# Attention on 64-row halves of the PE array, column tiles that interleave the causal work, and causal masks moved to VectorE and GpSimd

## The reference, cut to what matters

```python
scores = einsum('bqhd,bkhd->bhqk', q, k) / sqrt(8)     # F and H: every query sees every key
attn = softmax(scores); ctx = einsum('bhqk,bkhd->bqhd', attn, v)

attn = einsum('bhql,bkl->bhqk', q_lat, c_kv) / sqrt(8)  # L, causal
attn = where(tril, attn, -inf); attn = softmax(attn)
```

## Time and profile before

| | us |
|---|---|
| three runs | 3379.24, 3382.4, 3384.87; median 3382.4 |
| span of the profiled execution | 3382.5 |
| PE busy | 3032.9 (90%) |
| DVE busy | 2225.2 (66%) |
| ACT busy | 1668.8 (49%) |
| POOL busy | 168.7 (5%) |
| mean granted PE clock | 0.915 |

### The profile page before, as it was taken

How to read it: one execution, slowest core, us unless ns; L and a number is a source line. 1 busy time by engine, 2 the same in 40 slices (tenths; PEclk the granted TensorE clock), 3 DMA queues, 4 the chain that set the end, 5 groups by cost and what they waited for, 6 DMA issues and landing times. The chain is left out here.

```text
span 3382.5 us, 48839 instructions
## 1 busy us (share of the span) xinstructions
PE 3032.9 (90%) x14997; PEld 1205.9 (36%) x14997; DVE 2225.2 (66%) x4191; ACT 1668.8 (49%) x2007; POOL 168.7 (5%) x88
## 2 busy tenths in 40 slices
PE   6788859999999997997799999958999999998998
PEld 2787732222222223443233333322222222222443
DVE  5444459988889893223667666647989888894322
ACT  4212123666666665433255555531666666666333
POOL 1222220000000000001100000011000000000000
PEclk9888866999999997998699999975999999999899
DMA  1000010110011011120111111111010000110211
GB/s 37 1 0 0 0 61 11 29 29 19 27 29 29 17 30 32 69 69 12 59 32 39 30 30 41 30 32 59 15 30 29 29 19 28 29 29 21 76 56 31
DMA packets 75059, 105.46 MB, mean 31 GB/s; under 512 B 17334, under 2 KB 48016, under 8 KB 72433
## 3 DMA queue, kind: packets, MB, share of 16 engines
q1 hardware_dynamic: 71755, 100.97, 9.8%
q10 hardware_dynamic: 3104, 1.94, 0.2%
HBM read 68.72 MB, written 20.55 MB: 26 GB/s over the span
## 5 line engine op out<-in xcount | busy, mean ns | idle before, releaser
L466 DVE TENSOR_REDUCE Hmaxes<-Hm 128x1 f32<-128x512 f32 x1044 | 658.2, 685 | 95.6 <-PE Hm L392 95.0
L466 DVE TENSOR_REDUCE Fmaxes<-Fm 128x1 f32<-128x512 f32 x1044 | 658.1, 685 | 95.5 <-PE Fm L392 95.1
L447 ACT ACTIVATE Hprob<-Hs 128x1024 f32<-128x1024 f32 x512 | 498.5, 1021 | 242.3 <-PE Hs L357 240.7
L447 ACT ACTIVATE Fprob<-Fs 128x1024 f32<-128x1024 f32 x512 | 498.5, 1021 | 242.1 <-PE Fs L357 240.6
L466 DVE TENSOR_REDUCE Lmaxes<-Lm 128x1 f32<-128x512 f32 (+3 forms) x664 | 373.1, 605 | 179.0 <-PE Lm L392 105.3
L447 ACT ACTIVATE Lprob<-Ls 128x1024 f32<-128x1024 f32 (+7 forms) x384 | 293.1, 776 | 268.5 <-PE Ls L360 144.8
L392 PE MATMUL Hm<-Hka,Hqa 99*128 99x512 bf16 x1044 | 381.6, 404 | 27.4 <-DMA Hvh<-Hvstack 11.5
L392 PE MATMUL Fm<-Fka,Fqa 99*128 99x512 bf16 x1044 | 381.4, 404 | 26.8 <-DMA Fvh<-Fvstack 11.0
L357 PE MATMUL Fs<-Fqa,Fka 99*128 99x512 bf16 x1024 | 308.3, 385 | 1.6 <-ACT Fprob L447 1.2
L357 PE MATMUL Hs<-Hqa,Hka 99*128 99x512 bf16 x1024 | 308.2, 384 | 1.6 <-ACT Hprob L447 1.2
L374 PE MATMUL Ho<-Hprob,Hvh 128*32 128x512 f32 x2048 | 276.3, 612 | 0.6 <-ACT Hprob L447 0.6
(11 more groups left out here) (428 smaller groups left out, 2883.7 us busy)
## 6 DMA issues: line engine op xcount, KB each, us to landing
FEwb<-FE_weights SPq DMA_DIRECT2D x8, 1024.0 KB, 5.9
HEwb<-HE_weights SPq DMA_DIRECT2D x8, 1024.0 KB, 5.3
Fqa<-F_qparts SPq DMA_DIRECT2D x51, 96.0 KB
Fka<-F_kparts SPq DMA_DIRECT2D x51, 96.0 KB
Lqa<-L_qparts SPq DMA_DIRECT2D x51, 96.0 KB
Lka<-L_kparts SPq DMA_DIRECT2D x51, 96.0 KB
Hqa<-H_qparts SPq DMA_DIRECT2D x51, 96.0 KB
Hka<-H_kparts SPq DMA_DIRECT2D x51, 96.0 KB
```

Source lines behind the costliest of these rows:

```text
L447: nc.scalar.activation(prob[:, kt % PSLOTS, q0:q1], sps[SLOT_OF[kt, half]][:, q0 - half * 1024:1024], ACT.Exp, scale=SCALE).then_inc(expd, 1)
L466: nc.vector.reduce_max(maxes[:, qt, kb:kb + 1], src[:, 0:n], AX.X).then_inc(max_free, 1)
```

## The change

- **Layout.** The nine products of parts are split in two groups. `qa` and `ka` hold the first eight on 64 rows (8 x 8), once on partitions 0 to 63 and once on 64 to 127. New tiles `qx` and `kx` hold the ninth product (third part by third part) on 8 rows and the maximum's three rows from row 32 on (XROWS = 35), again in both halves. A head's loads become 17 DMAs (8 for q, 8 for k, one for the values), and `tops` issues 6 instead of 3. The rows of zeros for the maximum are no longer loaded.
- **Scores.** For a half of the queries, two passes over its banks: a 64-row matmul from `ka`/`qa`, then an accumulating 35-row matmul from `kx`/`qx`. Even banks use rows 0 to 63 of the array, odd banks rows 64 to 127. The number of score matmuls doubles. The mask matmul is gone.
- **Maxima.** One 64-row matmul with eight of the nine products; items alternate between the two halves of the array. The mask matmul is gone: on the diagonal DVE adds a constant row mask and takes the maximum in one instruction (`tensor_tensor_reduce`).
- **Causal mask of the weights.** POOL sets the weights ahead of the diagonal to zero in `prob` (`affine_select` on 128x128 fp32, once for a key tile), after the first exponential of that key tile; `weigh` waits for it (`cut`).
- **Causal weighing.** Column tile g serves the query tiles g, g+4, g+8, g+12 in place of bank g; the DMAs of `spread` put the queries back in order.
- **Order.** Within a key tile: an even number of items (about half), both halves of the next scores, the other items, the weighing. BEFORE is 2.
- **Constants.** Two masks of 128 columns are replaced by one of 512; two copies to bf16 are gone.

```diff
-MROW = 96
-KROWS = MROW + PARTS
+HALF = 64
+TOPROW = 32
+XROWS = TOPROW + PARTS
...
-    LOADS = 16 * (2 * PARTS + 2)
+    LOADS = 16 * (2 * 4 + 2 * 4 + 1)
...
     def load_q(sp, h, s):
-        for a in range(PARTS):
-            sp.dma_start(qa[a * PARTS * DH:(a + 1) * PARTS * DH, s, :], qscr[a, bass.ds(h * DH, DH), :].unsqueeze(1)
-                         .broadcast_to([DH, PARTS, T])).then_inc(loaded[s], 16)
-        sp.dma_start(qa[MROW:KROWS, s, :], zero_rows[0:PARTS, :]).then_inc(loaded[s], 16)
+        for r in (0, HALF):
+            for a, copies in ((0, 3), (1, 3), (2, 2)):
+                at = r + 3 * DH * a
+                sp.dma_start(qa[at:at + copies * DH, s, :],
+                             rows(qscr, a, h).unsqueeze(0).broadcast_to([copies, DH, T])).then_inc(loaded[s], 16)
+            sp.dma_start(qx[r:r + DH, s, :], rows(qscr, 2, h)).then_inc(loaded[s], 16)
...
-                nc.gpsimd.memset(qa[0:KROWS, :, :], 0.0).then_inc(filled, 1)
-                pool.wait_ge(filled, 1)
+                nc.gpsimd.memset(qx[:, :, :], 0.0).then_inc(filled, 1)
...
-                nc.gpsimd.memset(ka[0:MROW, :, :], 0.0).then_inc(filled, 1)
+                nc.gpsimd.memset(kx[:, :, :], 0.0).then_inc(filled, 1)
                 pool.wait_ge(filled, 3)
-                nc.gpsimd.memset(ka[MROW:KROWS, :, :], 1.0).then_inc(filled, 1)
+                for r in (0, HALF):
+                    nc.gpsimd.memset(kx[r + TOPROW:r + XROWS, :, :], 1.0).then_inc(filled, 1)
...
-    BEFORE = 1
+    BEFORE = 2
...
                     sp.wait_ge(max_free, count(h, "turn"))
-                    for a in range(PARTS):
-                        sp.dma_start(qa[MROW + a:MROW + a + 1, s, :].rearrange("o (t q) -> o t q", t=NT),
-                                     toprow[a * NT:(a + 1) * NT, :]).then_inc(top_in, 16)
+                    for r in (0, HALF):
+                        for a in range(PARTS):
+                            at = r + TOPROW + a
+                            sp.dma_start(qx[at:at + 1, s, :].rearrange("o (t q) -> o t q", t=NT),
+                                         toprow[a * NT:(a + 1) * NT, :]).then_inc(top_in, 16)
...
-                        for q0, q1 in blocks(kt, half):
-                            diag = causal and q0 == kt * P
-                            o = q0 - half * 1024
-                            last = nc.tensor.matmul(sps[slot][:, o:o + q1 - q0], ka[0:KROWS, s, kt * P:(kt + 1) * P],
-                                                    qa[0:KROWS, s, q0:q1], start=True, stop=not diag)
-                            if diag:
-                                last = nc.tensor.matmul(sps[slot][:, o:o + P], mask_kq[:, :], ident_bf[:, :],
-                                                        start=False, stop=True)
+                        for last_part in (False, True):
+                            for q0, q1 in blocks(kt, half):
+                                r = HALF * (q0 // BANK % 2)
+                                o = q0 - half * 1024
+                                kk, qq, n = (kx, qx, XROWS) if last_part else (ka, qa, HALF)
+                                last = nc.tensor.matmul(sps[slot][:, o:o + q1 - q0], kk[r:r + n, s, keys],
+                                                        qq[r:r + n, s, q0:q1], start=not last_part, stop=last_part,
+                                                        tile_position=(r, 0))
...
+                    if causal:
+                        pe.wait_ge(cut, h * NT + kt + 1)
...
+                            i0 = -((g - kt) // NB) if kt > g else 0
+                            if i0 == NB:
+                                continue
+                            last = nc.tensor.matmul(
+                                ops[VW * g:VW * (g + 1), i0 * P:BANK], weights,
+                                prob[:, kt % PSLOTS, :].rearrange("p (i g n) -> p i g n", g=NB, n=P)[:, i0:NB, g, :],
+                                start=(kt == 0), stop=(kt == NT - NB + g), tile_position=(0, VW * g))
...
-                    m = nc.tensor.matmul(out[:, 0:n], qa[0:KROWS, s, qt * P:(qt + 1) * P],
-                                         ka[0:KROWS, s, kb * BANK:kb * BANK + n], start=True, stop=not diag)
-                    if diag:
-                        m = nc.tensor.matmul(out[:, n - P:n], mask_qk[:, :], ident_bf[:, :],
-                                             start=False, stop=True)
+                    r = HALF * (j % 2)
+                    nc.tensor.matmul(out[:, 0:n], qa[r:r + HALF, s, qt * P:(qt + 1) * P],
+                                     ka[r:r + HALF, s, kb * BANK:kb * BANK + n], start=True, stop=True,
+                                     tile_position=(r, 0)).then_inc(max_in, 1)
...
-                        for k, part in enumerate((0, 1, "weigh")):
-                            for ahead, j in items[round(len(items) * k / 3):round(len(items) * (k + 1) / 3)]:
+                        first = (len(items) + 2) // 4 * 2
...
+                        maxima(items[:first])
+                        for half in range(2):
+                            if kt + 1 < NT:
+                                score(h, u, kt + 1, half)
                             elif not last:
-                                score(h + 1, (u + 1) % SLOTS, 0, part)
+                                score(h + 1, (u + 1) % SLOTS, 0, half)
+                        maxima(items[first:])
+                        weigh(h, u, kt)
...
+                    if causal and kb * BANK + n == (qt + 1) * P:
+                        dve.sem_inc(passed, 1)
+                        nc.vector.tensor_tensor_reduce(src[:, 0:n], src[:, 0:n], mask_row[:, BANK - n:BANK], 1.0, 2 * BIG,
+                                                       ALU.add, ALU.max, maxes[:, qt, kb:kb + 1]).then_inc(max_free, 1)
+                    else:
+                        nc.vector.reduce_max(maxes[:, qt, kb:kb + 1], src[:, 0:n], AX.X).then_inc(max_free, 1)
...
+            if causal:
+                @block.gpsimd
+                def _(pool):
+                    none = pool.to_reg(0.0)
+                    with pool.Fori(0, NH) as h:
+                        for kt in range(NT):
+                            pool.wait_ge(expd, 2 + h * NHALF + AHEAD[kt] + 1)
+                            pool.sem_inc(passed, 1)
+                            diag = prob[:, kt % PSLOTS, kt * P:(kt + 1) * P]
+                            nc.gpsimd.affine_select(diag, diag, [[1, P]], ALU.is_ge, none, base=0, channel_multiplier=-1)\
+                                .then_inc(cut, 1)
```

More of the change, by code:

```diff
@@ L75, in attention @@
     vstack = heads.enter_context(nc.sbuf_tensor(name + "vstack", [P, HEADS_PAD, NT, VW], F32))
-    qa = heads.enter_context(nc.sbuf_tensor(name + "qa", [P, SLOTS, T], BF16))
-    ka = heads.enter_context(nc.sbuf_tensor(name + "ka", [P, SLOTS, T], BF16))
+    qa, ka, qx, kx = (heads.enter_context(nc.sbuf_tensor(name + n, [P, SLOTS, T], BF16)) for n in ("qa", "ka", "qx", "kx"))
     topp = heads.enter_context(nc.sbuf_tensor(name + "topp", [P, P // NT, NT], BF16))
@@ L88, in attention, with rows @@
     loaded = [semaphore(nc, heads, f"{name}loaded{s}") for s in range(SLOTS)]
-    LOADS = 16 * (2 * PARTS + 2)
+    LOADS = 16 * (2 * 4 + 2 * 4 + 1)
+    def rows(scr, a, h):
+        return scr[a, bass.ds(h * DH, DH), :]
     def load_q(sp, h, s):
-        for a in range(PARTS):
-            sp.dma_start(qa[a * PARTS * DH:(a + 1) * PARTS * DH, s, :], qscr[a, bass.ds(h * DH, DH), :].unsqueeze(1)
-                         .broadcast_to([DH, PARTS, T])).then_inc(loaded[s], 16)
-        sp.dma_start(qa[MROW:KROWS, s, :], zero_rows[0:PARTS, :]).then_inc(loaded[s], 16)
-    def load_kv(sp, h, s):
-        for a in range(PARTS):
-            sp.dma_start(ka[a * PARTS * DH:(a + 1) * PARTS * DH, s, :], kscr[:, bass.ds(h * DH, DH), :]
-                         .rearrange("b d t -> d b t")).then_inc(loaded[s], 16)
+        for r in (0, HALF):
[4 more added lines that the diff above has]
+            sp.dma_start(qx[r:r + DH, s, :], rows(qscr, 2, h)).then_inc(loaded[s], 16)
+    def load_kv(sp, h, s):
+        for r in (0, HALF):
+            for a, parts in ((0, 3), (1, 3), (2, 2)):
+                at = r + 3 * DH * a
+                sp.dma_start(ka[at:at + parts * DH, s, :], kscr[0:parts, bass.ds(h * DH, DH), :]).then_inc(loaded[s], 16)
+            sp.dma_start(kx[r:r + DH, s, :], rows(kscr, 2, h)).then_inc(loaded[s], 16)
         sp.dma_start(vh[:, s, :], vstack[:, bass.ds(h, 1), :, :].rearrange("p h t d -> p (h t d)")).then_inc(loaded[s], 16)
@@ L277, in attention @@
         y_in = sem("y_in")
+        cut = sem("cut")
+        passed = sem("passed")
         def bank(c):
@@ L366, in weigh @@
                     pe.wait_ge(expd, 2 + h * NHALF + AHEAD[kt + 1])
+                    if causal:
+                        pe.wait_ge(cut, h * NT + kt + 1)
                     if kt == 0:
                         pe.wait_ge(out_sb, h + 1)
```

(19 more changed lines are left out.)

33 lines of the change are left out of this document (15 added, 18 removed).

## The result

| | before | after |
|---|---|---|
| median of the runs, us | 3382.3 (3379.2 to 3384.9) | 3454.0 (3444.6 to 3457.3) |
| ratio, 95% interval | | 1.0207 (1.0192 to 1.0222) |
| profiled execution: span, us | 3382.5 | 3455.6 |
| mean granted clock, share of full speed | 0.915 | 0.873 |

A forecast was written before the change was run, and what follows sets the result against it. PE was taken to bound the kernel, with DVE close behind. From 3382.5, F and H save 132, L saves 32 and the stretches before head 0 add 21: 3239.5, so 3240 (own case, chance 0.58), range 3140 to 3385.

The forecast's parts named there:

- the landing: In L, a head's load data was taken to arrive 2.2 us after the last issue, priced from the sums' DMA.
- L waits more: Rival: in L, DMAs at 0.86 and POOL at 1.37 make L lose 7 a head; 3388, chance 0.07.
- a wait of 1.2 for the sums: In L, DVE waits for sums read back behind the loads, so PE stands 1.2 a head with its banks full.
- The falling clock: Rival: L's new gaps hold PE's clock at 0.50, costing 17 a head or 255; about 3500, chance 0.05.
- Full overlap of pairs: Two matmuls on different row halves of PE's array run at the same time, a pair taking 0.217.
- the tile of 2.48: In F and H, a key tile falls from 2.83 to 2.48 us, saving 0.35, with PE and DVE coupled by three banks.
- the 132: F and H together gain 132, 66 a stage: 84 from shorter tiles less 18 charged for DVE's division and split maxima.
- 32 forecast: L as a whole gains 32: 2.1 a head, 30 for 15 heads, and 2 for the last.
- the forecast's waits, less the turn's: In L, a head waits 2.5 for loads, 1.2 for sums and 2.0 for POOL, while the turn's 1.67 goes.
- POOL's 2.0: In L, POOL's selection, taken as 0.4 us, delays weighings in eight tiles, 2.0 a head in all.
- 6.1 a head: L's net PE saving: weighing 3.9, mask matmuls 1.9 and maxima 2.0 gained, scores 1.7 lost.
- 18 x 0.22 = 3.9 a head: In L, interleaving cuts the widest column tiles' blocks from 58 to 40, at 0.22 each.

The follow-up runs named there:

- more work around the turn: Late-division kernel with four maxima instead of two before the turn in L and its third head asked for after 18 maxima instead of 14: 3208.0, ratio 0.9490.
- the late-division kernel: Changed kernel with channels outermost, L's third head asked for ten items later and L's division moved to three quarters of DVE's stream: 3217.1, ratio 0.9527.
- by banks: The late-division kernel with L's weighing put back on one 512-query bank a column tile, without interleaving: 3229.2, ratio 0.9547.
- the two waits moved: Channels outermost, with L's third head asked for later and its division moved later: 3217.1, or 3208.0 with more work around the turn.

## Why the prediction was wrong

**The step that failed is the landing.** "landing takes 2.2 (the sums' DMA, the nearest)" carried the price of one DMA over to loads that the diff lays out otherwise. The numbers that were bounded were those of SP's issues, and they came out right (11.4); the transfer behind them was given no bound. It took 9.1, and with the old order of dimensions 2.0. The rival "L waits more" went only as far as 0.86 for an issue, so nothing in the range held it; its own time, 3388, was already above the range's end of 3385. With the old order of dimensions, and nothing else changed, the time is 3274, inside the range.

**What the landing set off** was in the prediction for L only, as a wait of 1.2 for the sums. In F and H no cover was named for the sums' read-back, which stands behind the same loads; it cost 49 in F and 52 in H (764 against 715, 764 against 713). L lost 42 by it and the stretches ahead of head 0 29. The falling clock, a rival with 0.05, is part of these sums: it came in the waits or right after them (1.51 and 1.78 for a weighing then, at 0.50 and 0.56, with 1.00 ahead of them), so it is not counted as a cause of its own. In F PE is busy for 693 with the parts outermost and 673 with the channels, in the same matmuls, so some 20 of the 49 are matmuls that run longer (granted clock 0.91 against 0.94); the other 29 are standing.

**Right.** Full overlap of pairs, the tile of 2.48, DVE as the next bound, and F and H with channels outermost: 119 of the 132. Without the alternation of halves two matmuls run one behind the other, so the pairs are where this gain comes from; how much is theirs alone that run can't say, since its clock fell too. Ahead of head 0: 24 against 21.

**L was mis-sized even without the landing:** 5 gained, 32 forecast. Windows over all of L, before and with channels outermost:

```profile
1627.00:2206.00 579.00, 544.56 (x2988) 176.93 (x2989) 406.33 (x835) 281.44 (x375) 0.00 (x0) 0.94 0.11 32
```

```profile
1585.00:2159.00 574.00, 485.02 (x3625) 144.97 (x3626) 415.35 (x1102) 276.79 (x376) 70.13 (x240) 0.85 0.16 48
```

PE stands for 89 instead of 34, 55 more; the forecast's waits, less the turn's, make 60. Within these the loads took 3.3 a head instead of 2.5 (in the head shown the 17 issues took 12.6, not 11.2), and POOL's 2.0 came to nothing. The term that is off is PE's work. It was to fall by 6.1 a head, 92 over 15 heads, and fell by 60, at a granted clock of 0.85 instead of 0.94. With more work around the turn, where the clock is 0.93, PE is busy for 450, 95 less than before. So the 92 was about right at nearly the clock of before, and the lower clock behind the new waits, which the forecast's own case left out, took the rest: the same matmuls ran longer. It is alike with the "18 x 0.22 = 3.9 a head" of the interleaving: it saved PE 2.7 in the late-division kernel, and 3.5 where the clock is 0.93 (195 against 251 by banks, over 16 heads), while the kernel's time shows 0.5 to 0.8.

With the two waits moved L gains 72 to 80, so with these further edits it frees more of L than was forecast. The sum closes: 3239.5, and 13 less gained in F and H, 27 less in L, 3 more lost ahead, are 3283, the span of the profiled execution with channels outermost (3282.6; the median of its runs is 3274). What each of the masks and the maxima gives was not tried, nor what exactly bounds L at 30 a head: with more work around the turn PE is busy for 0.90 of it and DVE for 0.82, coupled by three banks.

## What to carry to other kernels

When a diff rewrites a DMA, read its outermost dimension and estimate the bytes that the busiest DMA engine gets (here 2.1 of 16 engines carried the end of the loads with 3 or 2 entries outermost, and 5.1 were busy in the middle with 8); number of issues and total bytes did not show it, as they are the same at 3454 and at 3274. In all 7% of this kernel's time, 3454 against 3208, hung on that and on the order of the steps behind it. When a transfer becomes late, list all that stands behind it on its issuing queue and move all of it: moving only the first waiter made the kernel slower. When an overlap has to be shown, take it away, and look at the clock in both: here it fell too, from 1.00 to 0.50 in a tile of F, so the run showed the overlap but not its size. When a saving on an engine doesn't come through in the time, compare the clock it was granted: here PE's work fell by 95 in L, nearly as forecast, at a granted clock of 0.93 and by 60 at 0.85.

## What the runs showed of the hardware that was not expected

- Loads with 3 or 2 entries in the outermost dimension kept 3.7 of 16 DMA engines busy in the middle of a head's loads and 2.1 at their end, at 25 GB/s each there (52 in all); the same rows with 8 outermost gave 5.1 in the middle, and landed 2.0 instead of 9.1 after the last issue.
- Two matmuls on rows 0 to 63 and 64 to 127 start together every 0.22, as one of 99 rows did alone.
- With all score and maximum matmuls on rows 0 to 63, PE was granted 0.50 while it was busy in all of a tile of 7.10; before, dense tiles with 99 rows had 1.00.
- DVE's masked maximum takes 287, 502 or 732 ns (least, median, most, at 128 to 512 columns), with 142 more for a read of the accumulator; POOL's selection over 128 x 128 takes 292.
- A shorter weighing came with a lower granted clock: over L 0.88 with the interleaving, 0.96 without it, and 26 of the 43 saved went back into scores and maxima.
